# Two of six tokenizer records as one-pass products of split halves, from the second image on

## The reference, cut to what matters

```python
xb = 2.0 * jnp.pi * xyz[..., None] * freq_bands            # xyz: (4, 3, 512, 192), 6 bands
feat = jnp.concatenate([jnp.sin(xb), jnp.cos(xb)], axis=-1).reshape(b, n, -1)
h = jnp.einsum('bnf,of->bno', feat, W)                     # 6912 features to 192
h = concat([cls_tok, h], axis=1)
h = h + attention(layernorm(h))
h = h + ffn(layernorm(h))        # shared expert and 2 of 8 routed experts
```

## Time and profile before

| | us |
|---|---|
| median of 3 runs | 560.63 (558.87 to 561.93) |
| the profiled execution | 560.72 |
| its span, first to last instruction | 558.9 |
| PE busy | 539.7 (97%) |
| PEld busy | 508.5 (91%) |
| DVE busy | 370.5 (66%) |
| ACT busy | 244.3 (44%) |
| POOL busy | 173.0 (31%) |

### The profile page before, as it was taken

One profiled execution on the slowest core, in us unless ns is written; L12 is line 12 of the kernel. 1 busy time (PEld: TensorE's weight loads), 2 busy tenths in 40 slices (PEclk: granted clock), 3 DMA queues, 4 the chain that ended last, 5 costly groups with the idle time before them and its releaser, 6 DMA issues.

```text
span 558.9 us, 9033 instructions
## 1 busy us (share of the span) xinstructions
PE 539.7 (97%) x3235; PEld 508.5 (91%) x3235; DVE 370.5 (66%) x1070; ACT 244.3 (44%) x343; POOL 173.0 (31%) x200
## 2 busy tenths in 40 slices
PE   5999999999999999999999999999799999999997
PEld 5998999899999899999989999879687899999875
DVE  8737787445788447978834975558788356666537
ACT  3465555753423763245474440362242134455410
POOL 6213224131344111855212550003210414444410
PEclk9999999999999899999999999899899999999999
DMA  8900076000100001110000110601103441531164
GB/s 330 335 21 20 20 245 205 20 23 7 39 2 19 20 0 29 59 58 0 1 1 10 37 41 1 226 10 40 40 0 114 134 158 50 164 102 53 52 216 139
DMA packets 23488, 42.49 MB, mean 76 GB/s; under 512 B 2502, under 2 KB 15044, under 8 KB 23348
## 3 DMA queue, kind: packets, MB, share of 16 engines
q1 hardware_dynamic: 19560, 33.31, 18.4%
q0 software_dynamic: 3472, 8.07, 4.1%
q10 hardware_dynamic: 412, 0.53, 0.4%
HBM read 31.74 MB, written 14.79 MB: 83 GB/s over the span
## 4 chain that ended last, share of the span: by engine, by line
PE 81%; DVE 11%; ACT 5%; issue 1%; DMA 1%; ACTq 0%; DVEq 0%
PE ps L1355 44%; PE ps L1557 4%; PE ps L1609 2%; PE ps L1611 2%; PE ps L1519 1%; PE ps L1522 1%; PE ps L1521 1%; PE ps L1520 1%; PE ps L1523 1%; PE ps L1587 1%; PE ps L1588 1%; PE ps L1589 1%; PE ps L1591 1%; PE ps L1590 1%; DMA r<-r 1%
## 5 line engine op out<-in xcount | busy, mean ns | idle before, releaser
L1355 PE MATMUL ps<-w_tok,feat 128*128 128x192 f32 x1728 | 290.4, 329 | 7.5 <-ACT feat L489 6.3
L1355 PEld LDWEIGHTS ps<-w_tok,feat 128*128 128x128 f32 x1728 | 283.9, 192 | 8.7 <-issue 8.7
L423 POOL TENSOR_SCALAR feat<-fx 128x512 int32<-128x512 f32 x108 | 90.9, 857 | 193.1 <-PE ps L1355 189.7
L498 ACT ACTIVATE feat<-feat 128x1536 f32<-128x1536 f32 x35 | 52.0, 1484 | 110.0 <-DVE feat L792 109.9
L788 DVE SCALAR_TENSOR_TENSOR feat<-fx,feat 128x512 f32<-128x512 f32 x105 | 76.0, 777 | 1.8 <-POOL feat L423 1.5
L501 ACT ACTIVATE feat<-feat,half_pi 128x1536 f32<-128x1536 f32 x35 | 54.6, 1561 | 0.0
L459 POOL DMA_INDIRECT ydram<-yr,xs x39 | 37.2, 955 | 54.6 <-DVE yr L1113 54.6
L453 POOL DMA_INDIRECT slots<-pay_a,posi x17 | 17.6, 1036 | 76.3 <-DVE posi L1040 72.9
L603 ACT ACTIVATE s_ring<-ps 128x512 f32<-128x512 f32 x24 | 14.4, 599 | 54.7 <-PE ps L1523 54.7
L1557 PE MATMUL ps<-w_down,hid_ring 128*128 128x192 f32 x192 | 36.2, 334 | 1.6 <-DVE H L1072 1.6
L792 DVE TENSOR_SCALAR feat<-feat 128x1536 int32<-128x1536 int32 x35 | 36.9, 1053 | 1.2
(11 more groups left out here) (305 smaller groups left out, 861.0 us busy)
## 6 DMA issues: line engine op xcount, KB each, us to landing
slots<-in_blank SPq DMA_DIRECT2D x1, 5031.0 KB, 19.5
w_tok<-in_wT SPq DMA_DIRECT2D x7, 576.0 KB, 8.8
fx<-in_xT SPq DMA_DIRECT2D x15, 256.0 KB, 2.6
xs<-slots SPq DMA_DIRECT2D x5, 645.0 KB, 6.2
yin<-ydram SPq DMA_DIRECT2D x8, 384.0 KB, 6.7
raw_a<-in_wea SPq DMA_DIRECT2D x4, 384.0 KB, 5.7
raw_b<-in_web SPq DMA_DIRECT2D x4, 384.0 KB, 6.3
w_tok<-in_wT SPq DMA_DIRECT2D x4, 288.0 KB, 7.5
```

The lines of the kernel that those rows point to most:

```text
L423: ins = pool.tensor_scalar(feat[:, k % SLOTS, i, :].bitcast(I32), x[:, x_block(k), :], f_col[:, fi:fi + 1], 1.0, ALU.mult, ALU.mult)
L498: act.activation(feat[:, k % SLOTS, 0:3, :], feat[:, k % SLOTS, 0:3, :], ACT.Sin, scale=TWO_PI).then_inc(sin_ready, 1)
L1355: ins = pe.matmul(ps[:, TOK[a % 2][t // 2], (t % 2) * D:(t % 2 + 1) * D], feat[:, k % SLOTS, i, t * P:(t + 1) * P], w_tok[:, k, i, :], sta ...
```

## The change

- Records 4 and 5 of groups 0 to 7, in images 2 to 4, are split. ACT copies the features to float32r (`feature_high`, into the free block X23[0]), POOL writes the differences over the features (`feature_low`). The weights of these records are split once, in image 1 (`weight_high` on ACT, `weight_low` on POOL), and kept in `w_r`, which lies over `w_tok`, the low and high halves of a record three places apart.
- TensorE (`record`) then does two products per tile: high features on [low weights | high weights], 384 columns, and low features on high weights, 192 columns. Low times low is left out. The first 192 columns of the bank gather the small sums, the second 192 all else.
- Each token tile has a bank of its own (0 to 3), the same ones for all images. Groups 0 and 8 go tile by tile, so that a tile's sum is complete, copied and free early (`tok_tile`, `h_tile`). In group 0 the split records come after all others, and the group waits once, ahead of its first product, for sines and cosines.
- `take_h` copies per tile: one copy for image 1, two for the others, the small sums into `xn`. In the sequence's count a >= 2 (images 2 to 4), DVE adds them to H (128x768) ahead of the layer norm.
- On POOL the scatters are spread: one tile in each of groups 6 to 8, tiles 3 and 4 in the next image, or after the loop.
- The descriptor scratch of POOL's transfers is set to 4096 bytes of each partition.

```diff
@@
-TOK = ((0, 1), (2, 3))
+NG3 = NG - 1
+R3 = 2
+TOK = (0, 1, 2, 3)
@@ POOL
+            def weight_low(k):
+                w0 = w_at(k)
+                pool.wait_ge(whi_ready, k + 1)
+                pool.wait_ge(tok_group, k + 1)
+                pool.tensor_tensor(w_r[:, w0 + 4:w0 + 6, :].rearrange("p i o -> p (i o)"),
...
+            def feature_low(a, k):
+                pool.wait_ge(fhi_ready, halves_before(a, k) + 1)
+                pool.tensor_tensor(f_lo[:, k % SLOTS, 6 - R3:6, :].rearrange("p i t -> p (i t)"),
+                                   feat[:, k % SLOTS, 6 - R3:6, :].rearrange("p i t -> p (i t)"),
+                                   f_hi[:, k % 2, :, :].rearrange("p i t -> p (i t)").bitcast(F32),
+                                   ALU.subtract).then_inc(flo_ready, 1)
@@
                     rounds(b, k)
+                    if b == 0 and k >= SLOTS:
+                        weight_low(k - SLOTS)
+                    if b == 1 and k < NG3 + SLOTS - NG:
+                        weight_low(NG - SLOTS + k)
+                    if b >= 1 and k >= 1:
+                        feature_low(b, k - 1)
+                    if b >= 3 and k == 0:
+                        for t in range(3, ranked(b - 2)):
+                            scatter(b - 2, t)
                     if b >= 2:
                         if k == 1:
                             second_payload(b - 1)
-                        for t in {6: (0,), 7: (1, 2), 8: (3, 4)}.get(k, ()):
-                            if t < ranked(b - 1):
-                                scatter(b - 1, t)
+                        if k >= 6:
+                            scatter(b - 1, k - 6)
@@ ACT
+            def feature_high(a, k):
+                if a >= 2 or k >= 2:
+                    act.wait_ge(tok_group, NG * a + k - 1 if k >= 2 else NG * (a - 1) + NG3 - 1 + k)
...
+                act.wait_ge(sin_ready, 2 * (NG * a + k) + 2)
+                act.activation(f_hi[:, k % 2, :, :].rearrange("p i t -> p (i t)"),
+                               feat[:, k % SLOTS, 6 - R3:6, :].rearrange("p i t -> p (i t)"),
+                               ACT.Copy).then_inc(fhi_ready, 1)
@@ take_h
+                for t in range(NT):
+                    if t < NT - 1:
+                        act.wait_ge(tok_tile, (NT - 1) * b + t + 1)
+                    else:
+                        act.wait_ge(tok_group, NG * (b + 1))
+                    ins = act.activation(H[:, b, t, :], ps[:, TOK[t], D:2 * D], ACT.Copy)
+                    if b >= 1:
+                        ins = act.activation(xn[:, t, :], ps[:, TOK[t], 0:D], ACT.Copy)
+                    ins.then_inc(h_tile if t < NT - 1 else h_ready, 1)
@@ ACT order
                 sines(b, 1)
+                feature_high(b, 1)
                 sines(b, 2)
                 attn1(b)
...
+                feature_high(b, 2)
                 sines(b, 3)
                 odds(b)
                 take_v(b, 0)
+                feature_high(b, 3)
                 sines(b, 4)
...
                 move_k(b)
+                feature_high(b, 4)
...
@@ DVE, attn0
+                    if a >= 2:
+                        dve.tensor_tensor(H[:, a - 1, :, :], H[:, a - 1, :, :], xn[:, :, :], ALU.add).then_inc(h_sum, 1)
+                        dve.wait_ge(h_sum, a - 1)
@@ TensorE
+            def record(a, k, i, t):
+                tokens = slice(t * P, (t + 1) * P)
+                out_ = ps[:, TOK[t], D:2 * D]
+                if halved(a, k, i):
+                    f = f_hi[:, k % 2, i - 6 + R3, tokens]
+                    pe.matmul(ps[:, TOK[t], 0:2 * D], f, w_r[:, w_at(k) + i:w_at(k) + i + R3 + 1:R3, :], start=False,
+                              stop=False, skip_group_check=True)
+                    return pe.matmul(out_, f_lo[:, k % SLOTS, i, tokens], w_r[:, w_at(k) + i + R3, :], start=False,
+                                     stop=False, skip_group_check=True)
+                return pe.matmul(out_, feat[:, k % SLOTS, i, tokens], w_tok[:, w_at(k) + i, :],
+                                 start=(k == 0 and i == 0), stop=(k == NG - 1 and i == 5), skip_group_check=True)
@@ project
+                if q >= 1 and k in (0, NG - 1):
+                    pe.wait_ge(sin_ready, 2 * q + 2)
+                    for t in range(NT):
+                        if k == 0 and t < NT - 1:
+                            pe.wait_ge(h_tile, (NT - 1) * (a - 1) + t + 1)
+                        if k == 0 and t == NT - 1:
+                            pe.wait_ge(h_ready, a)
+                        for i in range(6):
+                            if not halved(a, k, i):
+                                ins = record(a, k, i, t)
+                        if k == NG - 1 and t < NT - 1:
+                            ins.then_inc(tok_tile, 1)
+                    if k < NG3:
+                        pe.wait_ge(flo_ready, halves_before(a, k) + 1)
+                        for i in range(6 - R3, 6):
+                            for t in range(NT):
+                                ins = record(a, k, i, t)
...
+                    if halved(a, k, i) and i == 6 - R3:
+                        pe.wait_ge(flo_ready, halves_before(a, k) + 1)
                     for t in range(NT):
+                        ins = record(a, k, i, t)
@@ up_one
-                if q in (1, 2) and bank in TOK[1]:
+                if q == 0 and i == 0:
                     pe.wait_ge(h_ready, B)
@@
-    nc = bacc.Bacc("TRN2", target_bir_lowering=False, num_devices=1)
+    nc = bacc.Bacc("TRN2", target_bir_lowering=False, num_devices=1, dynamic_dma_scratch_size=4096)
```

More of the change, by code:

```diff
@@ L93, in build @@
         with ExitStack() as first:
-            w_tok = first.enter_context(nc.sbuf_tensor("w_tok", [P, NG, 2 * 3, D], F32))
+            w_tok = first.enter_context(nc.sbuf_tensor("w_tok", [P, NG3 * (6 + R3) + 6, D], F32))
             feat = first.enter_context(nc.sbuf_tensor("feat", [P, SLOTS, 6, T], F32))
             fx = first.enter_context(nc.sbuf_tensor("fx", [P, FX + (JC + 1) * T], F32))
+        with ExitStack() as rounded:
+            w_r = rounded.enter_context(nc.sbuf_tensor("w_r", [P, NG3 * (6 + R3) + 6, D], F32R))
+            f_lo = rounded.enter_context(nc.sbuf_tensor("f_lo", [P, SLOTS, 6, T], F32R))
         f_col = fx[:, 0:NF + 3]
@@ L195, in build, with w_at, halved, halves_before @@
         ps = ctx.enter_context(nc.psum_tensor("ps", [P, 8, 512], F32))
+        f_hi = X23[:, 0, :, :].rearrange("p (s i) t -> p s i t", s=2)
+        def w_at(k):
+            return (6 + R3) * k
+        def halved(a, k, i):
+            return a >= 1 and k < NG3 and i >= 6 - R3
+        def halves_before(a, k):
+            return NG3 * (a - 1) + k
         R_E, R_PHI, R_S, R_P, R_C, R_QK, R_K = range(7)
@@ L467, in _ @@
                             second_payload(b - 1)
-                        for t in {6: (0,), 7: (1, 2), 8: (3, 4)}.get(k, ()):
-                            if t < ranked(b - 1):
-                                scatter(b - 1, t)
+                        if k >= 6:
+                            scatter(b - 1, k - 6)
+            for t in range(3, ranked(B - 2)):
+                scatter(B - 2, t)
             second_payload(B - 1)
@@ L649, in _ @@
             sines(0, 1)
+            weight_high(0)
             sines(0, 2)
             attn1(0)
+            weight_high(1)
             sines(0, 3)
+            weight_high(2)
             act.wait_ge(consts_ok, 2)
@@ L659, in _ @@
             sines(0, 6)
+            weight_high(5)
             split_hi_piece(1)
             sines(0, 7)
+            weight_high(6)
             attn8(0)
             sines(0, 8)
+            weight_high(7)
             sines(1, 0)
+            feature_high(1, 0)
             router(0)
@@ L686, in _ @@
                 sines(b, 5)
+                feature_high(b, 5)
                 sines(b, 6)
+                feature_high(b, 6)
                 sines(b, 7)
                 attn6(b)
+                feature_high(b, 7)
                 sines(b, 8)
@@ L693, in _ @@
                     sines(b + 1, 0)
+                    feature_high(b + 1, 0)
                 take_h(b)
```

42 lines of the change are left out of this document (25 added, 17 removed).

## The result

The changed kernel takes 603.88 us (median of 6 runs, 602.41 to 604.87); the kernel before took 561.65 beside it. The ratio is 1.0762 [1.0737, 1.0788]: slower by 7.6%, where 554.1 was forecast and 561.0 was the upper end of the range. The profiled execution took 604.87 us against 560.72, so 44.2 us have to be found.

What follows compares the result with a forecast made beforehand. TensorE's own time in the tokenizer's float32 products was taken as the bound. From 560.7 us: -7.7 for products, +1.0 lost at attn3, +0.2 for a wait, together -6.5, giving 554.1 us; range 549.5 to 561, chance 0.60.

Steps and rivals of the forecast that it cites:

- Products: TensorE, tokenizer: 192 float32 products become float32r pairs, 0.285 us against 0.325, gaining 7.7 us, 0.32 a group.
- A: Rival, TensorE: the narrow product's weight load is cheap, pair 0.260 us, 10.1 us gained, 550.5 us; chance 0.10.
- C: Rival, TensorE: a 192-column float32r product costs the float32 one's 0.325 us, 33 us lost, 594 us; chance 0.12.
- D: Rival, TensorE: the two products are issued as several each; its chance is counted in that of C.
- What of the gain stays: TensorE's meetings: attn3 waits away 1.0 us of the gain; attn1, attn6 and attn8 have enough slack and keep it.
- The halves: ACT copies (1.1 us) and POOL subtractions (2.3 us, at most 3.4), 24 each, hide in idle time; nothing charged.
- Rival B: POOL's subtractions slow DVE's layer norms; attn1, attn3, attn6, attn8 wait, 12 meetings at 0.2 us; 559.5 us, chance 0.18.
- Small costs: Image 1's group 8 waits for cosines, 0.2 us; smaller descriptor scratch charged nothing, 1 us kept for the range.
- The weight halves in image 1: ACT 0.45 us and POOL about 0.9, eight times, were to go into idle places of both; nothing charged.
- Taking H: ACT's copies of H by tile end before project(b, 0) overwrites the banks; nothing charged.
- The clock: TensorE: one stretch at the lower 1.2 GHz level more or less, 1.8 us either way.

Runs made afterwards that it cites:

- experiment 1: The change with its low halves written by a second ACT copy instead of POOL's subtraction (not the true low features); 554.69 us, ratio 0.9926.
- experiment 4: Kernel before plus 24 times two plain POOL copies of 128x1024 on buffers nobody else uses, at the places of the change's subtractions; 573.54 us, ratio 1.0243.
- 5: The change with each of POOL's 24 feature subtractions cut into eight pieces of 128x128; 597.19 us, ratio 1.0657.
- 6: The change with the feature subtractions of all eight groups moved from POOL to DVE, behind the next group's remainders; 561.77 us, ratio 1.0034.
- 2: The change without high and low halves, every record one float32 product; banks, tile order and copies of H by tile kept; 559.7 us, ratio 1.0002.
- 7: The change with subtractions on DVE where it was idle, groups 3 and 5 left float32, weights split in image 2 by DVE; 557.74 us, ratio 0.9959.
- 8: Kernel of 7 with group 4 float32 too, group 6's subtraction behind group 7's remainders, a routing step moved behind attn8; 565.91 us, ratio 1.0107.
- 9: Kernel of 8 with the routing step (places) put back behind attn6; 556.32 us, ratio 0.9933.
- 10: Kernel of 8 in the same order, with its 15 feature subtractions and 5 of the weights on POOL instead of DVE; 592.4 us, ratio 1.0585.

## Why the prediction was wrong

**Products.** Right: 0.285 us a pair, and 0.32 us less a group (group 2 of image 3 takes 7.47 us from its first product to attn2b, and took 7.79 before). Rivals A, C and D fall with it.

**What of the gain stays.** Right for a kernel without POOL's subtraction: attn3 took back 0.9 us, attn6 and attn8 stayed without a wait (experiment 1).

**The halves.** Here it failed. The step is the one that ends in "So even the upper bound hides, with 3.4 us to spare", and that then counts as cost only what queues behind the subtraction on POOL. The duration was well bounded: 2.34 us at the shortest, 2.42 in the median and 2.65 in the mean, against 2.3 taken. And TensorE indeed had the low halves in time. But I asked only who waits for the result, and not who can't run meanwhile. Its cost is on DVE's side, 53 us of longer DVE instructions, and 33 us more of waits on TensorE.

**Rival B** named the mechanism and the places, and gave it 0.18 and 0.2 us a meeting. Its size was the mis-sized term: 12 x 0.2 = 2.4 us stood where 33.0 us of waits came (1.4 of them in image 1), with single waits of 5.3 and 6.0 us. They grew by 15.5 us at attn6, 10.4 at attn1, 1.8 at attn3, and by 4.0 at attn5 (L1566), which it didn't name; attn8, which it named, has none of them. The sentence that brought it down, that four-element steps are hardly slowed, had it backwards: a hold costs a short step as much as a long one, and a chain of twelve steps only offers it more places to strike. The range's upper end was made from this rival and fell with it.

The trace of the kernel before had the rows to see it. Timeline, start of image 3: L792 with POOL idle, the roundings with DVE on statistics, and then both at once.

```profile
168.31 0.65 POOL L440 COPY pay_a<-pack 128x4 int32<-128x4 int32 x1
...
170.27 0.96 DVE L792 TENSOR_SCALAR feat<-feat 128x1536 int32<-128x1536 int32 x1
171.59 2.02 POOL L423 TENSOR_SCALAR feat<-fx 128x512 int32<-128x512 f32 x3 [1.97 <-PE ps L1355]
...
179.39 2.85 POOL L423 TENSOR_SCALAR feat<-fx 128x512 int32<-128x512 f32 x3 [5.77 <-PE ps L1355]
179.69 1.34 DVE L792 TENSOR_SCALAR feat<-feat 128x1536 int32<-128x1536 int32 x1
```

L792 takes 0.96 us alone and 1.34 beside roundings; three roundings take 2.02 us alone and 2.85 beside it; and a POOL copy of four elements takes 0.65 us beside DVE's remainders, about as long as one of theirs (a copy of that size takes 0.18 us alone, in experiment 4). I read L423's mean of 0.857 us as "slow one another" and took it as a few tenths more, when it was the mean of alone and held. The steps L769 and L766 had means of 162 and 170 ns only because none of them met a rounding; L771, of the same chain, had one at 632 ns and a median of 163.

**Small costs.** The wait at group 8 of image 1, forecast as 0.2 us, is 0.24 us without halves (from the last narrow product at 77.77 to 78.01), but 0.83 in the changed kernel (78.67 to 79.50). The weight halves in image 1 were charged nothing and cost more: the second image starts at 86.7 to 87.4 us in the four kernels that split them there (the change, experiments 1, 5 and 6), and at 84.8 to 85.9 in the five of the same order that don't (2 and 7 to 10). In the mean that is 1.5 us. Experiment 1 carries it as well. A calmer clock hid it there: its trace has one stretch of 3.4 us at the lower level, where the kernel before has three, and that is worth up to 3.4 us. Taking H, charged nothing, has 0.4 us of waits in experiment 1. So it was partly luck that the time of experiment 1 came so near to the forecast. **The clock** was forecast as 1.8 us either way. It gave 15.3, and in the changed kernel it went with the waits: what was one term more was bound to the term that failed.

What was only argued: that the clock fell because TensorE waited. In the changed kernel each of the six stretches at the lower level begins during a wait of 3.5 to 6.0 us or up to 1.2 us behind one. Of the three before, only the last has such a wait near it (393.41 to 397.14, the stretch from 398.50); the other two came without. No run held the waits or the clock fixed.

## What to carry to other kernels

Before work goes to an idle POOL, look for the DVE instructions that read and write SBUF beside it, and price the work at its own length on DVE's chain, not only on its own. Compare single rows of one instruction with the other engine idle and busy; a mean mixes them. Here the subtraction was better on the busier engine, in its idle places and away from the chains with little slack.

## What the runs showed of the hardware

- While POOL computes on SBUF, an instruction of DVE with two inputs in SBUF, or a TENSOR_SCALAR on SBUF, stood until POOL's instruction was over: 2.92 us for a four-element step. It can stand through a run of POOL instructions: 4.89 us over a subtraction and three roundings, 3.95 us over eight pieces. One-input copies do it too (experiment 4). Statistics on SBUF went on undisturbed, and so did instructions that read PSUM (L991, 411 ns in the mean, and 410 before). Beside the scatter at 253.71 in the changed kernel (1.06 us) four-element steps kept their 0.16 us.
- It works both ways. In the changed kernel, POOL stood for DVE, and then DVE for POOL:

```profile
83.39 2.05 DVE L880 SCALAR_TENSOR_TENSOR feat<-fx,feat 128x512 f32<-128x512 f32 x3
83.83 3.83 POOL L463 TENSOR_TENSOR f_lo<-feat,X 128x1024 fp32r<-128x1024 f32 x1 [1.63 <-ACT X L570]
85.47 3.01 DVE L884 TENSOR_SCALAR feat<-feat 128x1536 int32<-128x1536 int32 x1
```

  The subtraction of 2.4 us takes 3.83, since the remainders end at 85.44, and L884 of 1 us then takes 3.01, since the subtraction ends at 87.66.
- The subtraction of two tensors of 1024 columns takes DVE 1.21 to 1.30 us in the mean (experiments 6 to 9), and POOL 2.65 in the change.
